# A GRU with expert-choice routing: another end of the threshold search

## The reference, cut to what matters

```python
# x: (16, 256, 512) f32, cond: (16, 512)
def cell(h, x):                              # GRU, 256 steps in order
    gi, gh = x @ W_ih + b_ih, h @ W_hh + b_hh
    r, z = sigmoid(i_r + h_r), sigmoid(i_z + h_z)
    n = tanh(i_n + r * h_n)
    return (1 - z) * n + z * h
hs = scan(cell, cond, x)                     # 16 x 256 tokens of 512
logits = hs @ router_w + router_b            # 4096 tokens, 16 experts
S = softmax(logits, -1)
G, idx = top_k(S.T, 256)                     # every expert takes its 256 best tokens
out = hs[idx] @ expert_w + expert_b          # one weight matrix for all experts
y = zeros.at[idx].add(G[..., None] * out)
result = x + y
```

## Time and profile before

| | |
|---|---|
| median of 3 runs | 1110.79 us (1110.76 to 1112.92) |
| profiled execution, its own time | 1113.21 us |
| its span in the trace | 1111.1 us |
| TensorE busy | 1096.1 us (99%) |
| VectorE busy | 838.6 us (75%) |
| ScalarE busy | 407.3 us (37%) |
| instructions | 62010 |
| granted clock of TensorE, mean | 0.996 |

### The profile page before, as it was taken

The page is one execution under the profiler, slowest core; times in us unless marked ns, Lnnn a source line. Parts: engine busy times, 40 slices in busy tenths (PEclk is TensorE's granted clock), DMA queues, the critical chain, the costliest instruction groups (busy, mean ns, idle before and its releaser), DMA issues.

```text
span 1111.1 us, 62010 instructions
## 1 busy us (share of the span) xinstructions
PE 1096.1 (99%) x27355; PEld 898.4 (81%) x27355; DVE 838.6 (75%) x4526; ACT 407.3 (37%) x1621; POOL 6.8 (1%) x31
## 2 busy tenths in 40 slices
PE   8999999999999999999999999999999999999988
PEld 5778888888888888888888888888888888888872
DVE  5777777777777777777777777777777777776877
ACT  2333333343343343343433333433333433334430
POOL 2000000000000000000000000000000000000000
PEclk8999999999999999999999999999999999999999
DMA  7311111001111110000000000000000000000329
GB/s 251 80 31 23 23 22 18 16 16 22 22 23 22 22 23 13 16 20 13 13 13 13 14 13 11 6 13 13 14 13 13 13 13 4 4 3 4 93 66 303
DMA packets 80306, 36.85 MB, mean 33 GB/s; under 512 B 70035, under 2 KB 70035, under 8 KB 80038
## 3 DMA queue, kind: packets, MB, share of 16 engines
q1 hardware_dynamic: 77696, 28.66, 10.8%
q10 hardware_dynamic: 2342, 4.24, 1.2%
HBM read 24.49 MB, written 8.39 MB: 30 GB/s over the span
## 4 chain that ended last, share of the span: by engine, by line
PE 95%; DVE 2%; DMA 1%; issue 0%; SPq 0%; ACT 0%; DVEq 0%
PE gates L588 60%; PE gates L525 26%; PE ffn_ps L631 5%; PE gates L631 5%; DMA whh<-in_L_cond_W_hh 1%; PE log_ps L645 1%; SPq L284 0%; PE log_ps L716 0%; DVE u L819 0%; DVE wih L951 0%; ACT th L412 0%; SPq L287 0%; DVE zT L826 0%; DVE tok L844 0%; PE gates L736 0%
## 5 line engine op out<-in xcount | busy, mean ns | idle before, releaser
L588 PE MATMUL gates<-whh,tok 128*16 128x192 f32 x16384 | 713.2, 326 | 2.7 <-DVE tok L844 2.6
L588 PEld LDWEIGHTS gates<-whh,tok 128*16 128x16 f32 x16384 | 553.5, 123 | 113.5 <-DVE tok L844 4.8
L412 ACT ACTIVATE th<-gates 128x128 f32<-128x128 f32 x512 | 140.1, 274 | 338.2 <-PE gates L588 338.2
L819 DVE SCALAR_TENSOR_TENSOR u<-th,gates 128x64 f32<-128x64 f32 x512 | 113.5, 222 | 191.8 <-ACT th L412 191.8
L417 ACT ACTIVATE n_t<-v 128x64 f32<-128x64 f32 x512 | 131.8, 258 | 277.8 <-DVE v L823 277.8
L525 PE MATMUL gates<-wih,xS 128*32 128x192 f32 x3024 | 145.9, 326 | 0.0
L835 DVE STREAM_TRANSPOSE nT<-n_t 128x64 f32<-128x64 f32 x512 | 123.7, 242 | 0.0
L826 DVE STREAM_TRANSPOSE zT<-th 128x64 f32<-128x64 f32 x512 | 121.8, 238 | 0.0
L823 DVE SCALAR_TENSOR_TENSOR v<-u,gates 128x64 f32<-128x64 f32 x512 | 113.0, 221 | 8.8
L525 PEld LDWEIGHTS gates<-wih,xS 128*32 128x32 f32 x3024 | 98.1, 110 | 23.1
L844 DVE SCALAR_TENSOR_TENSOR tok<-new_n,z_h 128x32 f32<-128x32 f32 x512 | 109.9, 215 | 8.7
(11 more groups left out here) (138 smaller groups left out, 531.6 us busy)
## 6 DMA issues: line engine op xcount, KB each, us to landing
x_in<-in_x SPq DMA_DIRECT2D x248, 32.0 KB, 2.2
xs<-in_x SPq DMA_DIRECT2D x16, 256.0 KB, 3.7
out<-tok SPq DMA_DIRECT2D x16, 256.0 KB, 4.1
out<-tok ACTq DMA_DIRECT2D x16, 256.0 KB, 4.1
wih<-in_L_cond_W_ih SPq DMA_DIRECT2D x4, 768.0 KB, 7.4
whh<-in_L_cond_W_hh SPq DMA_DIRECT2D x4, 768.0 KB, 13.6
whh<-in_x SPq DMA_DIRECT2D x12, 256.0 KB, 3.3
we<-in_L_ffn_expert_w SPq DMA_DIRECT2D x4, 256.0 KB, 2.8
```

What stands on the lines that cost most here:

```text
L412: nc.scalar.activation(th[a][:, :, :].rearrange("p g c -> p (g c)"), gates[t // S % PAIRS][a][:, R_:HN], ACT.Tanh, scale=0.5).then_inc(th_ ...
L588: mm = nc.tensor.matmul(gates[t // S % PAIRS][a][Q * j:Q * j + rows, R_:GC].rearrange("b (g k c) -> b g k c", g=G, k=KH), columns, by_tile ...
L819: V.scalar_tensor_tensor(u[a][:, :], th[a][:, 0, :], 1.0, ps[a][:, HN:GC], ALU.add, ALU.mult).then_inc(u_ready[a], 1)
```

## The change

It touches only the search and what follows.

- **Wide units**: every `expert` call of the search gets `widest=4`. The numbers of units change: softmax 21, rounds 10, at the passage 7 and 5, at the end 7 and 4, beside the ties 8.
- **32-column sums**: each 128x128 matmul with a mask, and those that make the weights, becomes four of 128x32, one for each group of 32 output partitions (`sum_by_expert`).
- **Counts over a threshold** move from VectorE to ScalarE (`count_beyond`, Sign with a bias `beyond`), with results `cnt_beyond` and places of their own in PSUM. VectorE makes the bias (`start_beyond`, `move_beyond`), and the targets are computed from the new count, after the first count of the lower half.
- **Sides of scores**: ScalarE writes `side` = Sign((score - threshold) x 2^64), -1, 0 or 1; VectorE makes `rank` = prefix - 8192 x side, so one comparison with `fit` chooses scores above and ties that fit, and leaves out those below.
- **Segment sums**: R is the difference of the running count at the ends of segments, in place of a reduction. The formula of `fit` takes three operations.
- **Choice by quarters**: comparison and product are done quarter by quarter in the order 2, 3, 0, 1; the weights of quarters 2 and 3 are copied and the first output is made, then the rest is chosen.
- `PSUM_PLACES` changes.

```diff
-    LAST_UNITS, SOFTMAX_UNITS, ROUND_UNITS, SHORT_UNITS = [3, 6, 6, 6], 20, 10, 4
+    LAST_UNITS, SOFTMAX_UNITS, ROUND_UNITS = [3, 6, 6, 6], 21, 10
+    BEYOND_UNITS, TIE_UNITS = [[7, 5], [7, 4]], 8
-    PSUM_PLACES = [0, 1, 2, 3, 4, 9, 14, 18, 22, 27, 31]
+    PSUM_PLACES = [0, 1, 2, 3, 4, 7, 12, 16, 21, 26, 31]
+    QUARTERS = [2, 3, 0, 1]
+    FAR = 8192.0
+    SCALE = 2.0 ** 64
@@ scalar
+            def count_beyond(half, key):
+                act.wait_ge(beyond_ready, half + 1)
+                nc.scalar.activation(junk[3], key, ACT.Sign, bias=beyond[:, :],
+                                     accum_out=cnt_beyond[:, half:half + 1]).then_inc(cnt_act, 1)
...
+                if r == UPPER_ROUNDS + 1:
+                    count_beyond(0, upper)
+                    act.wait_ge(key_ready, NG + 1)
                 count_third(r, upper if r <= UPPER_ROUNDS else lower)
...
+            act.wait_ge(edge_ready, 1)
+            nc.scalar.activation(side.rearrange(BY_TOKEN, b=B, g=NG), Sc.rearrange("p (g b t) -> p b g t", g=NG, b=B), ACT.Sign,
+                                 bias=edge[:, :], scale=SCALE).then_inc(side_ready, 1)
+            count_beyond(1, lower)
@@ tensor
+            def sum_by_expert(ps, of, mask=same_expert):
+                for j in range(J):
+                    mm = nc.tensor.matmul(ps[Q * j:Q * (j + 1), :], mask[:, Q * j:Q * (j + 1)], of,
+                                          start=True, stop=True, skip_group_check=True)
+                return mm
+            def sum_beyond(half, counted):
+                expert(BEYOND_UNITS[half][0], widest=4)
+                pe.wait_ge(cnt_act, counted)
+                sum_by_expert(cnt_beyond_ps[half], cnt_beyond[:, half:half + 1]).then_inc(cnt_all, 1)
+                expert(BEYOND_UNITS[half][1], widest=4)
...
             pe.wait_ge(R_ready, 1)
-            nc.tensor.matmul(R_total_ps, same_expert[:, :], R[:, :], start=True, stop=True)
-            nc.tensor.matmul(R_before_ps, before[:, :], R[:, :], start=True, stop=True).then_inc(R_summed, 1)
-            expert(ROUND_UNITS + SHORT_UNITS)
+            sum_by_expert(R_total_ps, R[:, :])
+            sum_by_expert(R_before_ps, R[:, :], before).then_inc(R_summed, 1)
+            expert(TIE_UNITS, widest=4)
+            for i, g in enumerate(QUARTERS):
+                pe.wait_ge(chosen_ready, i + 1)
+                for j in range(J):
+                    mm = nc.tensor.matmul(weight_ps[Q * j:Q * (j + 1), g * NI:(g + 1) * NI], chosen[:, g * P + Q * j:g * P + Q * (j + 1)],
+                                          group_of[:, :], start=True, stop=True, skip_group_check=True)
+                mm.then_inc(weight_done, 1)
             expert(NT * UNITS, widest=4)
@@ vector, between the halves
-            V.tensor_scalar(junk[0], upper, thr_upper[:, :], None, ALU.is_gt, ALU.add,
-                            accum_out=cnt[:, 0:1]).then_inc(cnt_own, 1)
...
             count(lower)
+            dve.wait_ge(cnt_all, UPPER_ROUNDS + 1)
+            V.tensor_scalar(target[:, 0:2], above_half.broadcast_to([P, 2]), -0.5, CAP - 0.5 * N, ALU.mult, ALU.add)
+            V.tensor_scalar(target[:, 2:3], above_half, -1.0, 2 * CAP - 2 * N, ALU.mult, ALU.add)
+            target_set = mark(V.tensor_scalar(need_base[:, :], above_half, -0.5, CAP - N, ALU.mult, ALU.add))
@@ vector, the end
+            V.tensor_scalar(edge[:, :], thr[:, :], -SCALE, None, ALU.mult).then_inc(edge_ready, 1)
             link(V.tensor_scalar(tie.rearrange(BY_TOKEN, b=B, g=NG), S_by_token, thr[:, :], None, ALU.is_equal))
+            link(V.tensor_tensor_scan(prefix, tie, zeros16[:, :], 0.0, ALU.add, ALU.add))
+            V.tensor_tensor(R[:, :], prefix_ends, prefix_starts, ALU.subtract).then_inc(R_ready, 1)
+            dve.wait_ge(side_ready, 1)
+            mark(V.scalar_tensor_tensor(rank, side, -FAR, prefix, ALU.mult, ALU.add))
+            dve.wait_ge(cnt_all, ALL_ROUNDS + 2)
+            mark(V.tensor_scalar(need[:, :], cnt_beyond_ps[1], -0.5, need_base[:, :], ALU.mult, ALU.add))
...
+            link(V.tensor_tensor(others[:, 1:], R_total_ps, R[:, :], ALU.subtract))
+            link(V.tensor_tensor_scan(scan_b[:, :], zeros[:, :], others[:, 0:SEG], need[:, 0:1], ALU.add, ALU.subtract))
+            link(V.tensor_tensor(fit[:, :], scan_b[:, :], R_before_ps, ALU.subtract))
...
+            compare(QUARTERS[0])
+            compare(QUARTERS[1])
+            choose(QUARTERS[0])
+            choose(QUARTERS[1])
+            compare(QUARTERS[2])
+            compare(QUARTERS[3])
+            take_weights(slice(0, 2))
+            add_x(0)
+            choose(QUARTERS[2])
+            choose(QUARTERS[3])
+            add_x(1)
+            take_weights(slice(2, 4))
+            for i in range(2, NT):
+                add_x(i)
```

More of the change, by code:

```diff
@@ L719, in _ @@
             pe.wait_ge(masks_ready, 1)
-            for r in range(1, UPPER_ROUNDS + 1):
+            for r in range(1, UPPER_ROUNDS):
                 sum_counts(r, r)
[L722 to L727, removed]
@@ L738, in _ @@
-            mm.then_inc(weight_done, 1)
+                expert(ROUND_UNITS, widest=4)
+            sum_counts(UPPER_ROUNDS, UPPER_ROUNDS)
+            sum_beyond(0, UPPER_ROUNDS + 1)
+            for r in range(UPPER_ROUNDS + 1, UPPER_ROUNDS + LOWER_ROUNDS):
+                sum_counts(r, r + 1)
+                expert(ROUND_UNITS, widest=4)
+            sum_counts(UPPER_ROUNDS + LOWER_ROUNDS, UPPER_ROUNDS + LOWER_ROUNDS + 1)
+            sum_beyond(1, UPPER_ROUNDS + LOWER_ROUNDS + 2)
+            pe.wait_ge(R_ready, 1)
@@ L1026, in _ @@
+            V.tensor_tensor(R[:, :], prefix_ends, prefix_starts, ALU.subtract).then_inc(R_ready, 1)
+            dve.wait_ge(side_ready, 1)
+            mark(V.scalar_tensor_tensor(rank, side, -FAR, prefix, ALU.mult, ALU.add))
             dve.wait_ge(cnt_all, ALL_ROUNDS + 2)
-            V.tensor_scalar(need[:, :], cnt_ps[:, 0:1], -1.0, float(CAP), ALU.mult, ALU.add)
+            mark(V.tensor_scalar(need[:, :], cnt_beyond_ps[1], -0.5, need_base[:, :], ALU.mult, ALU.add))
+            for p in range(4):
+                dve.wait_ge(xs_loaded[p], 8 * 16)
@@ L1029, in _ @@
             dve.wait_ge(R_ready, 1)
             dve.wait_ge(R_summed, 1)
[L1031 to L1046, removed]
@@ L1052, in _, with take_weights @@
                                 ALU.mult).then_inc(chosen_ready, 1)
[L1054 to L1059, removed]
+            def take_weights(places):
+                dve.wait_ge(weight_done, places.stop)
+                g = min(QUARTERS[places])
+                link(V.tensor_copy(weight[:, g:g + 2, :], weight_ps.rearrange("p (g i) -> p g i", g=NG)[:, g:g + 2, :]))
@@ L1063, in _ @@
                     dve.wait_ge(ffn_done, n + 1)
-                g, i = n // 8, 2 * (n % QUAD) + n // QUAD % 2
-                V.scalar_tensor_tensor(tile(n), tile(n) if n < IN_PSUM else bank(n)[:, :], weight[:, g, i:i + 1],
+                g, column = n // 8, 2 * (n % QUAD) + n // QUAD % 2
+                V.scalar_tensor_tensor(tile(n), tile(n) if n < IN_PSUM else bank(n)[:, :], weight[:, g, column:column + 1],
                                        xs_tile(n),
                                        ALU.mult, ALU.add).then_inc(out_ready, 1)
+            compare(QUARTERS[0])
[12 more added lines that the diff above has]
+                add_x(i)
 _INS = ["x", "cond_2048", "L0_cond_W_ih", "L0_cond_W_hh", "L0_cond_b_ih", "L0_cond_b_hh", "L0_ffn_router_w",
```

81 lines of the change are left out of this document (55 added, 26 removed).

## The result

| | before | after |
|---|---|---|
| median of 13 runs | 1110.86 us (1108.89 to 1115.37) | 1108.13 us (1107.41 to 1109.07) |
| ratio | | 0.9972, 95% interval 0.9963 to 0.9981 |
| profiled execution: time, span | 1113.21, 1111.1 | 1108.13, 1106.0 |
| first to last sum of a round | 39.78 us | 33.50 us |
| last sum to TensorE's last matmul | 32.74 us | 32.88 us |

The kernel is faster, by 3.1 us from the ratio (0.28% of 1110.86; 2.1 to 4.1 by its interval) where 4.9 were forecast; 1108.13 lies inside the range of 1103.5 to 1109.2, but outside the forecast's own 1104.6 to 1107.3, next to the 1108.4 of rival (a). The two profiled executions differ by 5.1 us, nearly what the sum gave for them. The spread of the times fell from 6.5 us to 1.7. All medians here are those of fast executions; the one slow one, 2348.97 us in the last version of experiment 5, is left aside.

What follows compares the result with a forecast made beforehand. TensorE, busy 99% of the span, was taken as the bound. Search 6.1 us less, minus 1.2 for tail and stores, gave 4.9: median 1110.79 to 1105.9 us, own range 1104.6 to 1107.3, 8 in 10 within 1103.5 to 1109.2.

Steps and rivals of the forecast that it cites:

- 32-column sums: Search rounds: a sum costs TensorE 0.11 us, not 0.24; VectorE becomes the bound at 2.32 us a round.
- rival (a): Search: gaps belong to each instruction border, not the time between borders; 2.8 us stay, 1108.4 us; chance 0.18.
- What bounds: Whole kernel: TensorE is busy 99% of the span; only its work, its idle time or what follows its last matmul counts.
- three stretches of the sum: After softmax: search 39.78 us, end of search 8.09, tail 24.67, then stores; search wins 6.1 us, tail and stores lose 1.2.
- the prediction's own signs: Wrong if the last sum is not 6 us sooner, or the last landing does not move with it by 4 us or more.
- From the profiled execution to the median: Difference of 4.9 us computed on the profiled execution (1113.21 us), carried over to the median of 1110.79 us.
- Wide units and the gaps: Search: 128 pairs last 6.1 us rather than 4.1, so instruction fetches land in time; gaps fall from 4.27 us to 0.3.
- (b): Search: gaps are not fetches but go with the loads of x; 4.27 us stay, 1109.9 us; chance 0.07.
- Rival (c): Search: a sum's four matmuls don't overlap, 0.48 us more on VectorE's path, round 2.74, 1112.4 us; chance 0.06.
- Passage: Upper to lower half of the search: 0.85 us off, 3.07 us between sums; first lower round 0.2 longer, 2.52.
- End of the search: After the last sum: first add at 6.35 us instead of 8.40; TensorE idles 0.7 and 1.4, starts the tail at 7.9.
- Stores: Tail: stores start 2 us sooner, but waits for tiles 25 and 26 empty the DMA queues; 1.2 us lost.

Runs made afterwards that it cites:

- experiment 5: Late loads of x cut to 8 partitions each: in the kernel before, 1109.59 us; in the changed kernel with narrow search units, 1110.38 us.
- experiment 3: The kernel before with wide units (widest=4) in the search alone: 1109.36 us, ratio 0.9978.
- (4): The changed kernel with narrow units in the search (widest=4 taken away): 1112.14 us, ratio 1.0007.
- experiment 6: The changed kernel with each round's sums as one 128x128 matmul again: 1109.25 us, ratio 0.9973.
- experiment 2: The kernel before, no edit, third and fourth profiled executions: 1112.81 and 1112.73 us; its table sets six executions of that kernel together.
- experiment 7: The changed kernel with 6 expert units between the weights of the second and third quarter: 1107.47 us, ratio 0.9961.
- Experiment 8: The changed kernel with PSUM_PLACES 0, 1, 2, 3, 8, 13, 18, 23, 28, 30, 31: 1106.20 us, ratio 0.9952.

## Why the prediction was right, and where it was off

**What bounds.** Right. The three stretches of the sum came out one by one: search 33.50 us (forecast 33.43 and 0.3 of gaps), last sum to TensorE's end 32.88 (33.2; it was 32.74), and the span ends 5.1 us sooner in the profiled execution, where 4.9 were forecast. By the prediction's own signs it holds: the last sum comes 6.1 us sooner and the end moves by 5.1. But both are counted from one execution with long gaps; against the second one they are 2.1 us and 0.8.

**From the profiled execution to the median.** This step failed, and it accounts for the difference of 4.9 and 3.1. The text noted that the first profile's time was 2.4 us over the median and carried the difference over all the same. The surplus was not spread over the kernel: most of it was the very term that the change takes away. Gaps of 4.27 us in that execution, 0.28, 3.20 and 3.95 in three others; 1108.13 / 0.9972 = 1111.24, 2.6 us over the 1108.65 of an execution with none. These 2.6 us are gaps and late stores together; with them in place of 4.27 the sum is 3.2 instead of 4.9. In later batches the kernel before was up to 4.1 us over 1108.65, so the gain depends on the batch that it is measured in. That 1108.13 still fell inside the stated range is owed to the room left for rival (a), whose mechanism was wrong.

**Wide units and the gaps.** The mechanism was right: the gaps stand at borders of 128 pairs, they are gone with wide units (experiment 3), come back with narrow ones (4), and each ends 1.2 to 1.6 us after a late transfer (5). Against rival (a), no border costs anything when pairs are used slowly; against (b), the loads of x are unchanged in experiment 3. The use time of 128 pairs was misread: 81 pairs in 2.43 us make 3.84 us, not the 4.1 of the text, whose 127 pairs between two gaps include idle time. And the recurrent loop does not cross borders at the same rate, as the argument against (a) had it: its 6317 pairs between 250 and 500 us make 5.1 us for 128, with no gap. It speaks for the pace rather than against (a). The Trainium skill, Runtime: NRT & Kernel Launch, section Instruction fetch mechanics, has fetches hidden by the pace of issue; here four executions of one program differ by 4 us at the borders of 256 instructions, so the measurement decides against it for a stream of such pairs. Wide units alone were worth 2.4 us (experiment 3), in another batch than the 3.1 us of the whole.

**32-column sums.** Right, also in that VectorE becomes the bound, by little: mostly 2.27 and 2.37 us in turn, mean 2.31 to 2.32. By the sum of TensorE alone they would have been 2.27. Rival (c) is out, at its 2.74 us as well as at the 2.80 that TensorE's 2.16 and 0.64 would have made; experiment 6 puts the worth at 0.09 us a round, 1.1 in all.

**Passage.** 3.3 us instead of 3.07 between the sums, 0.6 less than before and not 0.85: VectorE reads the last upper sum 0.32 us after its start, and not 0.15, and it takes 0.96 us from the start of the key (1048.43) to the first count (1049.39), where it took 0.81 before (1050.90 to 1051.71). The first lower round is 2.38 and not 2.52, so half of this is made up.

**End of the search.** TensorE waits 0.70 us for the last count (0.7) and 1.28 for the third quarter (1.4); weights and first add come 0.2 and 0.3 us sooner than forecast. The change wins 2.4 us on VectorE's side up to the first add, and hardly any of it reaches TensorE, which starts the units of its tail 7.5 us after the last sum (forecast 7.9) instead of 8.1, but with 118 of them and not 114.

**Stores.** Rightly seen: holes before tiles 25 and 26 (2.68 and 1.36 us), and queues that run full to the end. The cost was of the forecast's size: 5.82 us from the last add to the end of the span, against 4.7 to 5.7 in the six executions of experiment 2. One execution would not show this; the kernels of experiments 4, 5 (narrow units) and 6, with the same places, have 5.9 to 6.1, so it is some 0.8 us on average. The kernel of experiment 7, where the hole before tile 25 is 1.64 us, has 5.1. Experiment 8 gets 1.8 us from another order. Against the second execution of the kernel before, nearly without gaps, TensorE ends 1.9 us sooner (1100.16, 1102.07) and the span only 0.8 (1106.0, 1106.8): 1.1 us of what search and passage won was given back to the stores.

## What to carry to other kernels

Before a difference from one profile is carried over to the median, ask which term of the profile holds the surplus of that execution; if it is the term that the change removes, take a second profile or price it by the median. A change may be worth more for the instructions it saves than for its busy time: wide units saved 1% of TensorE's work in the search, 0.4 us, and some 2 us of waits. In a tail where stores run at full rate, put finished tiles ahead of those that must be waited for; the hole in the queue comes back at the end.

## What the runs showed of the hardware

The same program had 0.3 to 4.3 us of gaps at borders of 256 instructions of TensorE's queue when 128 pairs of weight load and matmul were used in 3.84 us (the one before the last 27 pairs of the fifth round and the one before the last 26 of the last in three executions); a version that used 128 pairs in 3.5 us had 4.1. There was none at 6.1 us in the search with wide units, and none at 5.1 in the recurrent loop. The transfer of the next 256 instructions started 0.3 to 2.8 us after a border, took 0.9 to 1.4, and in all 17 gaps TensorE went on 1.2 to 1.6 us after its end. Shrinking transfers of 256 KB beside them took away 1.2 us (by the ratio) to 2.2 us (by the medians) of about 3.1 at 3.84 us, and 1.8 of 4.0 at 3.5 (2.6 by the ratios).

A sum's result was seen by VectorE 0.23 us after its start where narrow units stood before it (1062.62 to 1062.85), and 0.33 us (1060.25 to 1060.58) where the group before last was 512 columns wide, which makes the rounds alternate by 0.1 us. Four 128x32 sums of 3 columns between 128x32 matmuls took 0.09 us a round less than one 128x128 sum.
